# One block instead of three for a fused residual kernel with attention: shared PSUM banks and SBUF regions, first queries ahead of the first scores

## The chip, the cores and the metric

The kernel runs on one core of a Trainium2 chip. The metric is device time in microseconds (us) of one execution. Engines are named as in the profile: PE (TensorE matmuls), PEld (its weight loads), DVE (VectorE), ACT (ScalarE), POOL (GpSimd), SP (SyncE, which only issues DMAs here; "SPq" in the rows). "Hi" and "lo" are the two fp32r parts of an fp32 number; a product is three matmuls (hi·hi, lo·hi, hi·lo), summed in PSUM.

## The reference, cut to what matters

`x` is 8 × 128 × 512 in fp32. Four residual stages follow one another. Indices (`itok...`) pick an adapter for each of the 8 batches.

```
x += x @ W0[a0[b]].T                                   # L0: 512 x 512 of its own per batch
q,k,v = x @ wq,wk,wv + (x @ A[a1[b]]) @ B[a1[b]]       # L1: 32 query heads, 8 kv heads, D = 128
q,k = rope(q), rope(k)
p = softmax(where(causal & mask, q k^T / sqrt(128), min))
o = p v
x += o @ wo + (o @ ao[a1[b]]) @ bo[a1[b]]
x += (x @ B2[a0[b]].T) @ A2[a0[b]].T                   # L2, rank 16
x += x @ W3.T + b3 + 2 * (x @ A3[a3[b]]) @ B3[a3[b]]   # L3, rank 16
```

## The kernel before, in words

*Block one* (L0, and the first tiles of V): per batch, PE transposes x, multiplies by W0, and from batch four on (`LAG`) also does the V tile of an earlier batch with `v_tile` (L176-182), 8 tiles in all. It ends with PE at 97 us. In its last part ACT and DVE make the sine, cosine and mask tables.

*Block two* (L650-800, the projections): a loop over tiles n = 8..31, then four more. Tiles 8 to 15 are the second half of V, 16 to 31 are K (`project`, L70-83), 32 to 35 the queries of the first head for the first half of the tokens. A tile is 128 × 512 results in one of four banks `ps_p[n % 4]`. For a V tile, ACT copies the bank to `v_hi[n % 2]` (L733), DVE subtracts to get `v_lo[n % 2]` (L755), and SP stores both to HBM (`store_v`, L173). ACT may write `v_hi[n % 2]` again only once the stores of tile n-2 have landed (`v_out`). In the same loop ACT and DVE split the next block of weights out of `raw_w` and `raw_b` (L727, L729, L743, L167), and SP, behind the store of tile 11, loads `raw_w` for the block after (L148). For K and query tiles DVE multiplies by cosine and sine and POOL adds the two (L782) to `kr`, which SP stores to `k_rot`, or to `qt`. In the order of SP, behind the store of K tile 16, stand the loads of `wo` and of `ao` for head 0 (L646, 8 DMAs). POOL gathers the rows of `bo` and of L3's B (L773, L775; 16 DMAs) ahead of its first rotation.

*Block three* (attention and the rest): `over_heads` runs head 0, a hardware loop over heads 1 to 6, and head 7 written out as `last`. A head has 8 slots, one per batch. In a slot PE does the scores of its batch (L1403), a tile of queries (L76-81), the transposes of the previous batch's probabilities (`turn`, L1411), `outputs` of the batch before that (L1441-1445: o times wo and ao), and `values` of the previous batch (L1419-1421). DVE takes the scores' maxima (L1256), ACT the exponentials (L1055), POOL divides by the sums and adds the rotations of the queries; ACT and DVE split the transposed probabilities (`pt`: L1035, L1224) and the values' result (`ot`: L1041, L1228). `outputs(t)` waits for `ot(t)`.

In the last head the first four slots still make queries. In slots 4 to 7 `prepare(b)` works for the late stages: in slot 4 PE multiplies the L2 and L3 adapters (`m`) and DVE masks the result with `same` (`m_sb`, L1303), then in slot 5 PE folds it back and DVE adds it to `l3a_sel`, in slot 6 PE multiplies L2's A by W3 (`ps_c`). `m_sb` waits for `rows_in`, which counts `same` and the 8 `l2b_rows`. These two are loaded to `wo_raw`, which is free only late, and SP issues them behind 8 × (`l2b_sel`, `l2a_sel`) and 8 × `l3a_sel` (L981-994). After the last head: the sums `axo_n` are transposed (`turn_axo`, L1501), bo, L2 and L3 are multiplied, and x is stored.

## Time and profile before

| what | value |
|---|---|
| median of 3 runs | 783.78 us (782.24 to 786.15) |
| profiled execution, its own time | 783.69 us |
| its span, first to last instruction | 782.0 us |
| mean granted TensorE clock | 0.976 of full |
| PE busy | 719.9 us (92% of the span), 4388 matmul instructions |
| DVE / ACT / POOL busy | 537.2 / 327.0 / 291.0 us |
| mean share of the DMA engines, by the page's strip | from 0 to 9 tenths; 105 GB/s over the span |

The difference between 783.69 and 782.0 us lies around the span. PE is the engine with the most busy time; the 62 us in which it is not busy lie in a few places, which the views by stretch and the timelines of single engines show. A clock of 1.0 in a stretch is 2.4 GHz for PE, 0.5 is 1.2 GHz.

### The profile page before, as it was taken

To read this page: it belongs to the slowest core of one execution; us is meant where nothing else is said; L and a number is where in the kernel's file an instruction comes from. 1 tells how busy PE (TensorE), PEld (TensorE's weight loads), DVE (VectorE), ACT (ScalarE), POOL (GpSimd) and SP (SyncE) were. 2 spreads that over 40 slices of the span, in tenths; PEclk is the share of its full clock that TensorE was granted. 3 is DMA by queue.
4 is the path that set the end of the run, shared out by engine and by line. 5 is a ranking of instruction groups with operands and counts; after the bars stand their busy time and mean duration, and the time that the engine had idled before them with its cause. 6 is when DMAs were issued, how large, how long until landed. Compare 5 with 4: busy or idle time off the path is not lost.

```text
span 782.0 us, 14163 instructions
## 1 busy us (share of the span) xinstructions
PE 719.9 (92%) x4388; PEld 636.3 (81%) x4388; DVE 537.2 (69%) x1455; ACT 327.0 (42%) x980; POOL 291.0 (37%) x245
## 2 busy tenths in 40 slices
PE   3799958999789999999999999999999999968798
PEld 2678746887579989989998998998999899958686
DVE  4699434888586777677677768767676776834575
ACT  3563513110254454354445445436444543524332
POOL 3353122445362263344236235335423623423121
PEclk9999979999899999999999999999999999998999
DMA  7963277764014034023122403302412110527511
GB/s 229 347 215 123 81 202 225 224 251 170 19 55 128 2 128 129 2 74 134 47 57 70 127 0 127 127 0 74 134 47 73 54 47 7 123 55 97 67 42 67
DMA packets 60971, 81.81 MB, mean 105 GB/s; under 512 B 20438, under 2 KB 38102, under 8 KB 57350
## 3 DMA queue, kind: packets, MB, share of 16 engines
q1 hardware_dynamic: 60018, 80.04, 34.0%
q0 software_dynamic: 768, 1.25, 0.7%
q8 instruction: 18, 0.29, 0.2%
q14 instruction: 19, 0.16, 0.1%
q10 hardware_dynamic: 148, 0.07, 0.0%
HBM read 66.39 MB, written 15.47 MB: 105 GB/s over the span
## 4 chain that ended last, share of the span: by engine, by line
PE 65%; SPq 4%; DVE 3%; issue 2%; ACT 0%; DMA 0%; ACTq 0%
PE ps_wide L1441 8%; PE ps_wide L1445 8%; PE ps_wide L1443 7%; PE ps_q L76 7%; PE ps_q L78 7%; PE ps_q L77 7%; PE ps_s L1403 6%; PE ps_t L1411 3%; PE ps_o L1420 2%; PE ps_o L1419 2%; PE ps_o L1421 2%; PE ps_q L81 2%; PE ps_wide L1548 1%; PE ps_wide L1550 1%; PE ps_wide L1549 1%
## 5 line engine op out<-in xcount | busy, mean ns | idle before, releaser
L1170 POOL TENSOR_TENSOR prob<-prob,rinv 128x512 f32<-128x512 f32 x64 | 66.7, 1042 | 198.7 <-DVE rinv L1275 198.7
L1055 ACT ACTIVATE prob<-sm,nmax 128x128 f32<-128x128 f32 x256 | 99.8, 391 | 73.5 <-DVE nmax L1256 73.4
L1441 PE MATMUL ps_wide<-wt_x,v_hi 128*128 128x272 f32 x512 | 113.9, 304 | 10.4 <-DVE v_lo L1228 8.2
L1163 POOL TENSOR_TENSOR qt<-qc,qs 128x512 f32<-128x512 f32 x60 | 77.5, 1292 | 107.4 <-DVE qs L1211 107.4
L1445 PE MATMUL ps_wide<-wt_x,v_lo 128*128 128x272 f32 x512 | 107.5, 292 | 0.0
L1443 PE MATMUL ps_wide<-wt_lo,v_hi 128*128 128x240 f32 (+1 forms) x512 | 103.9, 285 | 0.0
L1041 ACT ACTIVATE v_hi<-ps_o 128x512 fp32r<-128x512 f32 x64 | 38.1, 596 | 155.2 <-PE ps_o L1421 155.2
L76 PE MATMUL ps_q<-x1t_hi,blk_hi 128*128 128x512 f32 x240 | 100.8, 420 | 0.0
L78 PE MATMUL ps_q<-x1t_hi,blk_lo 128*128 128x512 f32 x240 | 95.8, 399 | 0.0
L77 PE MATMUL ps_q<-x1t_lo,blk_hi 128*128 128x512 f32 x240 | 95.6, 398 | 0.0
L1441 PEld LDWEIGHTS ps_wide<-wt_x,v_hi 128*128 128x128 f32 x512 | 81.0, 192 | 14.4 <-DVE v_lo L1228 9.3
L1211 DVE TENSOR_TENSOR qs<-ps_q,sin_t 64x512 f32<-64x512 f32 x120 | 82.7, 689 | 3.7
L1443 PEld LDWEIGHTS ps_wide<-wt_lo,v_hi 128*128 128x128 f32 x512 | 81.8, 192 | 0.0
L1445 PEld LDWEIGHTS ps_wide<-wt_x,v_lo 128*128 128x128 f32 x512 | 80.6, 193 | 0.0
L1256 DVE CUSTOM_DVE_ANT_0 sm<-ps_s,maskbias 128x128 f32<-128x128 f32 x256 | 59.0, 286 | 29.6 <-issue 29.0
L1403 PEld LDWEIGHTS ps_s<-kt,qt 128*128 128x128 f32 x512 | 67.2, 193 | 11.4 <-issue 6.4
L1403 PE MATMUL ps_s<-kt,qt 128*128 128x128 f32 x512 | 68.4, 277 | 5.2 <-PEq L673 5.2
L1035 ACT ACTIVATE v_hi<-ps_t 128x512 fp32r<-128x512 f32 x64 | 38.2, 598 | 43.6 <-PE ps_t L1411 43.6
L1235 DVE TENSOR_TENSOR res<-ps_wide,res 128x272 f32<-128x272 f32 x128 | 50.0, 432 | 8.4 <-PE ps_wide L1445 8.4
L78 PEld LDWEIGHTS ps_q<-x1t_hi,blk_lo 128*128 128x128 f32 x240 | 45.6, 190 | 10.9
L1224 DVE TENSOR_TENSOR v_lo<-ps_t,v_hi 128x512 fp32r<-128x512 f32 x64 | 44.1, 689 | 14.0 <-ACT v_hi L1035 13.5
L77 PEld LDWEIGHTS ps_q<-x1t_lo,blk_hi 128*128 128x128 f32 x240 | 45.9, 191 | 8.5
(216 smaller groups left out, 1530.4 us busy)
## 6 DMA issues: line engine op xcount, KB each, us to landing
wo_raw<-in_L_cond_wo_l SPq DMA_DIRECT2D x8, 1024.0 KB, 4.8
raw_w<-in_L_cond_wq_l SPq DMA_DIRECT2D x8, 1024.0 KB, 5.2
raw_b<-in_L_cond_bq SPq DMA_DIRECT2D x64, 128.0 KB, 2.8
w_raw<-in_L_cond_weight_t SPq DMA_DIRECT2D x7, 1024.0 KB, 6.6
v_hi_d<-v_hi SPq DMA_DIRECT2D x16, 256.0 KB, 2.2
v_lo_d<-v_lo SPq DMA_DIRECT2D x16, 256.0 KB, 2.7
k_rot<-kr SPq DMA_DIRECT2D x16, 256.0 KB, 2.7
kt<-k_rot SPq DMA_DIRECT2D x16, 256.0 KB, 2.6
```

The source lines that it names most:

```text
L76: pe.matmul(bank[:, :], w_hi[:, k, cols], x1t_hi[:, k, tok], start=(k == 0), stop=False)
L77: pe.matmul(bank[:, :], w_hi[:, k, cols], x1t_lo[:, k, tok], start=False, stop=False)
L78: pe.matmul(bank[:, :], w_lo[:, k, cols], x1t_hi[:, k, tok], start=False, stop=False)
L1055: e = act.activation(prob[i][:, h, :], sm[:, h, :], ACT.Exp, bias=nmax[i][:, h:h + 1], scale=-1.0, accum_out=rsum[i][:, h:h + 1])
L1163: pool.tensor_tensor(qt[:, half, h, :], qc[:, :], qs[:, :], ALU.add).then_inc(q_done, 1)
L1170: pool.tensor_tensor(prob[i][:, :, :], prob[i][:, :, :], rinv[i][:, :].unsqueeze(2).broadcast_to([P, G, T]), ALU.mult).then_inc(prob_done, 1)
L1211: dve.tensor_tensor(qs[to:to + 64, :], ps_q[i][at:at + 64, :], sin_t[to:to + 64, tok], ALU.mult).then_inc(q_mult, 1)
L1256: m = dve.tensor_tensor_reduce(out=sm[:, h, :], in0=ps_s[i][:, h, :], in1=maskbias[:, b, :], scale=-1.0, scalar=3.0e38, op0=ALU.add, op1=A ...
L1403: mm = pe.matmul(ps_s[b % 2][:, h, :], qt[:, half, h, at:at + T], kt[:, b * T:(b + 1) * T], start=True, stop=True)
L1441: pe.matmul(ps_out[i][:, :], ot_hi[:, q], wo_x[:, h, wide], start=(h == 0), stop=False)
L1443: pe.matmul(bank, ot_hi[:, q], wo_lo[:, h, cols], start=False, stop=False)
L1445: mm = pe.matmul(ps_out[i][:, :], ot_lo[:, q], wo_x[:, h, wide], start=False, stop=(h == G - 1))
```

## The change

The three blocks become one. No engine waits for the others at the two seams; semaphores stand where a bank or a region passes from one use to the next.

- *Banks.* There are eight banks `bank[0..7]`. Stage one has `ps_x` = banks 0, 1 and `ps_y` = banks 2, 3; the projections' `ps_p` are banks 2, 3, 0, 1; attention has its scores in 4, 5, the transposes in 6, values in 7, queries in `ps_y` and outputs in `ps_x`.
- *SBUF.* Tiles that lived in different blocks share regions: `rot` (six tiles of 128 × 512) holds causal and mask tables, then k_cos, k_sin and kr, then attention's qc, qs, sm and prob, and in the end `axo_n`; `qt` lies where W0's raw weights were; `kt` and the values in the low and high parts of the K weights; `bo_raw` in one of the `blk_b`, the adapters of the late stages in `raw_b`.
- *Queries first.* In slot 0 of head 0, PE does the first tile of `queries` ahead of `scores(0)`; in all other slots the order stays.
- *Moved DMAs.* `ao` of head 0 is loaded behind the last rotated query tile, not behind K tile 16. `same` is loaded once at the start of the program, by POOL. In the last head SP issues `l2a` and `l3a` first (8 pairs), then bo's rows, then `l2b_sel` and `l2b_rows`.
- *Moved arithmetic in the last head.* `m` goes from slot 4 to slot 5 on PE, `m_sb` likewise on DVE, and waits for `same` alone; the fold goes from slot 5 to slot 7 on PE and behind the last `pt` on DVE. The memset of `axo_n` (L1292) goes from the start of attention on DVE to slot 4 of the last head. `l3a_hi` and `l2b_hi` go on ACT behind the heads, and their low parts with them.

The core of the diff (names and uses around it are left out where they only follow):

```diff
-        with ExitStack() as c:
-            k_cos = [sb(c, f"k_cos{i}", [P, HT]) for i in range(2)]
-            ps_p = [ps(c, f"ps_p{i}", [P, GW]) for i in range(4)]
-            with nc.Block() as block:
+            rot = sb(c, "rot", [P, 6, HT])
+            bank = [ps(c, f"bank{i}", [P, 512]) for i in range(8)]
+            ps_x, ps_y, ps_v = bank[0:2], bank[2:4], bank[5]
+            ps_p = ps_y + ps_x
+            v_bank = [ps_v] * LAG + [ps_p[n % 4] for n in range(LAG, B)]
+            ps_q, ps_t, ps_o, ps_wide = ps_y, bank[6], bank[7], ps_x
+            axo_n = rot[:, 0:2, :].rearrange("p i (b q a r) -> p (i b) q a r", q=4, a=2, r=R)
...
                         if n == VU:
                             load_wo(sp, 0)
-                            load_ao(sp, 0, 0)
-                            load_ao(sp, 0, 1)
...
+                    sp.wait_ge(k_done, VU + G)
+                    load_ao(sp, 0, 0)
+                    load_ao(sp, 0, 1)
...
                             if blk == 1:
+                                act.wait_ge(v_ready, UNITS)
...
                     def prepare(b):
                         if b == HALF:
-                            dve.wait_ge(rows_in, 16 * (B + 1))
-                            dve.wait_ge(m_ready, 1)
-                            dve.tensor_tensor(m_sb, ps_m, same, ALU.mult).then_inc(m_done, 1)
+                            dve.wait_ge(q_done, QUERIES)
+                            dve.memset(axo_n[:, :, :, :, :], 0.0).then_inc(axo_zeroed, 1)
                         elif b == HALF + 1:
                             dve.wait_ge(l2a_hi_done, 1)
                             dve.tensor_tensor(l2a_lo, l2a_sel[...], l2a_hi.bitcast(F32), ALU.subtract)
-                            dve.wait_ge(fold_ready, 1)
-                            dve.tensor_tensor(l3a_sel[...], by_batch(ps_fold[...]), l3a_sel[...], ALU.add)
+                            dve.wait_ge(same_in, 16)
+                            dve.wait_ge(m_ready, 1)
+                            dve.tensor_tensor(m_sb, ps_m, same[:, :], ALU.mult).then_inc(m_done, 1)
```

**How the rows move.** On PE around the first seam, the end of V tile 7, the join (branches) and the first matmuls of V tile 8 of the kernel before:

```order
L181 MATMUL ps_y1<-blk_hi0,x1t_lo 128x512
L182 MATMUL ps_y1<-blk_b0,axt_v 128x512
L248 UNCONDITIONAL_BRANCH
L784 UNCONDITIONAL_BRANCH
L179 MATMUL ps_p0<-wt_x,x1t_hi 128x512
```

The same place in the changed kernel (ps_y1 is bank1 there, ps_p0 is bank2):

```order
L172 MATMUL bank1<-blk_hi0,x1t_lo 128x512
L173 MATMUL bank1<-blk_b0,axt_v 128x512
L170 MATMUL bank2<-wt_x,x1t_hi 128x512
L171 MATMUL bank2<-wt_lo0,x1t_hi 128x512
L172 MATMUL bank2<-wt_x,x1t_lo 128x512
```

Both branches are gone, and tile 8 stands directly behind tile 7. On PE around the second seam, the end of the last projection (query tile 35), the join, and slot 0 of head 0, before:

```order
L78 MATMUL ps_p3<-x1t_hi,blk_lo0 128x512
L81 MATMUL ps_p3<-axt_q,blk_b0 128x256 x2
L673 UNCONDITIONAL_BRANCH
L1383 UNCONDITIONAL_BRANCH
L1403 MATMUL ps_s0<-kt,qt 128x128 x4
L76 MATMUL ps_q0<-x1t_hi,blk_hi0 128x512
```

The changed kernel there; bank2 is the query tile of slot 0, bank4 and bank5 the scores of slots 0 and 1 (`wt_lo1` holds kt), bank3 the query tile of slot 1:

```order
L72 MATMUL bank2<-x1t_hi,blk_lo0 128x512
L75 MATMUL bank2<-axt_q,blk_b0 128x256 x2
L1397 MATMUL bank4<-wt_lo1,qt 128x128 x4
L1397 MATMUL bank5<-wt_lo1,qt 128x128 x4
L70 MATMUL bank3<-x1t_hi,blk_hi0 128x512
```

The 13 matmuls of slot 0's query tile moved ahead of `scores(0)`, and follow the last projection with no join between. On DVE in slot 4 of the last head, before (`v_lo0` and `v_lo1` are the low parts of `pt` and `ot`, the line with `wo_raw` is `m_sb`):

```order
L1224 TENSOR_TENSOR v_lo0<-ps_t,v_hi0 128x512
L1235 TENSOR_TENSOR res<-ps_wide0,res 128x272
L1235 TENSOR_TENSOR res<-ps_wide1,res 128x272
L1303 TENSOR_TENSOR wo_raw<-ps_q0,wo_raw 128x128
L1228 TENSOR_TENSOR v_lo1<-ps_o,v_hi1 128x512
L1253 MEMSET gate 128x1
```

And in the changed kernel:

```order
L1012 TENSOR_TENSOR v_lo0<-bank6,v_hi0 128x512
L1023 TENSOR_TENSOR res<-bank0,res 128x272
L1023 TENSOR_TENSOR res<-bank1,res 128x272
L1089 MEMSET rot 128x1024
L1016 TENSOR_TENSOR v_lo1<-bank7,v_hi1 128x512
L1041 MEMSET gate 128x1
```

The low part of `ot` (L1228, now L1016) no longer stands behind `m_sb`, but behind the memset of `axo_n`.

## Rows read from the trace of the kernel before

**Rows 1.** Windows by stretch: start:end, length, busy of PE, PEld, DVE, ACT, POOL, clock, DMA share, GB/s.
```profile
97.00:107.00 10.00, 0.36 (x2) 0.21 (x2) 3.21 (x4) 1.42 (x4) 0.00 (x0) 0.67 0.80 233
...
227.00:687.00 460.00, 459.89 (x3019) 418.46 (x3018) 334.08 (x1067) 210.92 (x706) 186.03 (x155) 1.00 0.24 75
```

**Rows 2.** Timeline of PE at the first seam: start, duration, instruction, [idle before <-releaser].
```profile
96.55 0.40 PE L181 MATMUL ps_y<-blk_hi,x1t_lo 128*128 128x512 f32 x1
96.79 0.40 PE L182 MATMUL ps_y<-blk_b,axt_v 128*128 128x512 f32 x1
106.82 0.77 PE L179 MATMUL ps_p<-wt_x,x1t_hi 128*128 128x512 f32 x1 [9.64 <-PEq L248]
...
110.72 0.40 PE L179 MATMUL ps_p<-wt_x,x1t_hi 128*128 128x512 f32 x1
```

**Rows 3.** Timeline of SP in the projections (DMA issues).
```profile
100.12 4.95 SPq L154 DMA_DIRECT2D raw_b<-in_L_cond_bk  x8
...
122.25 0.37 SPq L173 DMA_DIRECT2D v_hi_d<-v_hi  x1
123.22 0.57 SPq L148 DMA_DIRECT2D raw_w<-in_L_cond_wk_l  x1
...
143.79 4.46 SPq L646 DMA_DIRECT2D ao_raw<-in_L_cond_ao_l  x8
```

**Rows 4.** Stores of v_lo, 105 to 132 us, then the one at 105.9.
```profile
DMA to landing us min/median/max: 2.6/4.1/7.5
...
DMA to landing us min/median/max: 4.9/4.9/4.9
```

**Rows 5.** Timeline of ACT, the copy of V tile 14; POOL, its first gather.
```profile
133.25 0.60 ACT L733 ACTIVATE v_hi<-ps_p 128x512 fp32r<-128x512 f32 x1 [5.20 <-DMA v_lo_d<-v_lo]
...
108.57 0.51 POOL L773 DMA_DIRECT2D bo_sel<-in_L_cond_bo  x1 [15.99 <-issue]
```

**Rows 6.** Timeline of PE, K tile 16 and a later K tile.
```profile
135.29 0.50 PE L76 MATMUL ps_p<-x1t_hi,blk_hi 128*128 128x512 f32 x1 [2.36 <-DVE blk_b L167]
...
185.94 0.49 PE L76 MATMUL ps_p<-x1t_hi,blk_hi 128*128 128x512 f32 x1 [1.54 <-DVE blk_b L167]
```

**Rows 7.** Timeline of PE in the last head: outputs, then the matmul after them.
```profile
702.28 0.82 PE L1441 MATMUL ps_wide<-wt_x,v_hi 128*128 128x272 f32 x2 [5.75 <-DVE v_lo L1228]
...
707.83 1.10 PE L1480 MATMUL ps_q<-wo_raw 128*128 128x128 f32 x8
...
722.39 0.52 PE L1441 MATMUL ps_wide<-wt_x,v_hi 128*128 128x272 f32 x2 [2.45 <-DVE v_lo L1228]
...
731.40 0.75 PE L1501 MATMUL ps_q<-ident,axo_n 128*128 128x128 f32 x4 [3.85 <-DVE axo_n L1321]
```

**Rows 8.** Timeline of PE at the second seam and in slots 0 and 1.
```profile
197.95 0.40 PE L81 MATMUL ps_p<-axt_q,blk_b 128*128 128x256 f32 x2
203.53 1.20 PE L1403 MATMUL ps_s<-kt,qt 128*128 128x128 f32 x4 [5.18 <-PEq L673]
...
217.25 0.47 PE L1419 MATMUL ps_o<-v_hi 128*128 128x512 f32 x1 [2.39 <-DVE v_lo L1224]
...
222.31 0.50 PE L1441 MATMUL ps_wide<-wt_x,v_hi 128*128 128x272 f32 x2
```

**Rows 9.** Timeline there: POOL's last rotation, DVE's memset, rotation and next maxima.
```profile
200.60 1.26 POOL L782 TENSOR_TENSOR qt<-k_cos,k_sin 128x512 f32<-128x512 f32 x1 [1.76 <-DVE k_sin L766]
...
204.06 0.91 DVE L1292 MEMSET axo_n<- 128x1024 f32 x1 [0.16 <-issue]
...
212.74 0.06 DVE L1253 MEMSET gate<- 128x1 f32 x1
```

**Rows 10.** Timeline of SP in the last head, and of DVE at m_sb.
```profile
679.32 0.56 SPq L985 DMA_DIRECT2D l2a_sel<-in_L_cond_A_l  x1
...
682.81 7.96 SPq L988 DMA_DIRECT2D l3a_sel<-in_L_cond_lora_As_l  x8
...
701.34 0.29 DVE L1303 TENSOR_TENSOR wo_raw<-ps_q,wo_raw 128x128 f32<-128x128 f32 x1 [6.90 <-DMA wo_raw<-in_L_cond_B]
```

More of the change, by code:

```diff
@@ new lines, in program @@
+            same = sb(c, "same", [P, P])
+            gate = sb(c, "gate", [P, 1])
+            nmax = [sb(c, f"nmax{i}", [P, G]) for i in range(2)]
+            rsum = [sb(c, f"rsum{i}", [P, G]) for i in range(2)]
+            rinv = [sb(c, f"rinv{i}", [P, G]) for i in range(2)]
+            xt = sb(c, "xt", [P, 4, KC * T], F32R)
+            wt_hi1 = sb(c, "wt_hi1", [P, KC, HID], F32R)
+            wt_lo1 = sb(c, "wt_lo1", [P, KC, HID], F32R)
+            w0_raw = [qt[:, i, :, :] for i in range(2)]
@@ L210, in program @@
-            ps_at = ps(c, "ps_at", [P, 3, T])
+            rot_flat = rot[:, :, :].rearrange("p i t -> p (i t)")
+            a_raw = rot_flat[:, 0:4 * KC * 3 * R].rearrange("p (i k n r) -> p i k n r", i=4, k=KC, r=R)
+            causal = rot[:, 2, 0:T]
+            mask_u8 = rot[:, 3, 0:NT // 4].bitcast(U8)
+            small = blk_b[1][:, :, :].rearrange("p c n -> p (c n)")
+            A_COLS = KC * 3 * R
+            a_hi, a_lo = ([small[:, (2 * j + i) * A_COLS:(2 * j + i + 1) * A_COLS].rearrange("p (k n r) -> p k n r", k=KC, r=R)
+                           for i in range(2)] for j in range(2))
@@ new lines, in program @@
+            kv_v_hi = sem(c, "v_hi_done2")
+            kv_v_lo = sem(c, "v_lo_done2")
+            scaled = sem(c, "scaled")
+            k_mult = sem(c, "k_mult")
+            k_done = sem(c, "k_done")
+            k_out = [sem(c, f"k_out{i}") for i in range(2)]
+            BLOCKS = 2 * VB
+            VU = VB * UNITS
+            N0 = UNITS
+            wq_raw, bq_raw, wq_hi, wq_lo, bq_pack = raw_w, raw_b, blk_hi[0], blk_lo[0], blk_b[0]
+            wo_x, wo_hi, wo_lo = wt_x, blk_hi[1], blk_lo[1]
@@ new lines, in program, with load_late @@
+            nar_ready = sem(c, "nar_ready")
+            h_hi_done = sem(c, "h_hi_done")
+            h_lo_done = sem(c, "h_lo_done")
+            late_hi_done = sem(c, "late_hi_done")
+            late_lo_done = sem(c, "late_lo_done")
+            wide_ready = sem(c, "wide_ready")
+            y_done = sem(c, "y_done")
+            y_out = sem(c, "y_out")
+            QUERIES = B * (KVH - 1) + HALF
+            def load_late(dma, src, at, done):
+                for quad in range(4):
+                    row = 2 * R * quad + at
+                    dma.dma_start(late_raw[row:row + R, :, :], src.rearrange("b r n -> r b n")).then_inc(done, 16)
@@ new lines, in by_batch, with of_nar, flat, ao_of @@
+            def by_batch(tile):
+                return tile.rearrange("p k (b r) -> p b k r", r=R)
+            def of_nar(tile, which):
+                return tile[:, :, :, which, :].rearrange("p b k r -> p (b k) r")
+            def flat(tile):
+                return tile[:, :, :, :].rearrange("p b k r -> p (b k) r")
+            def ao_of(b, part):
+                at = part * R + b % 2 * (2 * R + HID)
+                return wo_x[:, :, at:at + R]
+            def over_heads(eng, slots):
+                slots(0, True, False)
+                with eng.Fori(1, KVH - 1) as g:
+                    slots(g, False, False)
+                slots(KVH - 1, False, True)
@@ L415, in _ @@
+                    for b in range(B):
+                        sp.wait_ge(y_done, b + 1)
+                        sp.dma_start(out[b], x_row(b)).then_inc(y_out, 16)
+                    sp.wait_ge(y_out, 16 * B)
                 @block.scalar
@@ L501, in _ @@
+                    x2t(0)
+                    act.wait_ge(late_in, 64)
+                    act.wait_ge(c_in, 64)
+                    late_part(0)
+                    for b in range(B):
+                        if b == 0:
+                            axo_part(1)
+                        if b + 1 < B:
+                            x2t(b + 1)
+                        narrow(b)
+                        if b + 1 < B:
+                            late_part(b + 1)
                 @block.vector
@@ new lines, in turn_ax @@
+                    def turn_ax(b):
+                        pe.wait_ge(axn_done, 4 * b + 4)
+                        if b == 0:
+                            pe.wait_ge(ident_ready, 1)
+                        else:
+                            pe.wait_ge(axt_done, 3 * b)
+                        for n in range(3):
+                            mm = pe.matmul(ps_at[:, n, :], axn[b % 2][:, n, :, :, :].rearrange("p a b r -> p (a b r)"),
+                                           ident_r[:, :], start=True, stop=True)
+                        mm.then_inc(axt_ready, 1)
```

1172 lines of the change are left out of this document (538 added, 634 removed).

## The prediction, made before the changed kernel was run

> **What bounds the kernel now.** I read the windows by stretch first, then the timelines of PE, SP, DVE, ACT and POOL around the stretches in which PE is idle. In the loop over heads PE is busy 459.89 of 460 us, and DVE, the next engine, 334.08 [rows 1]: there only PE's own work counts, and the change leaves it as it is. In the 10 us at the first seam PE is busy 0.36 us [rows 1], and its next matmul has stood idle for 9.64 us behind a branch [rows 2]. At the second seam it is 5.18 us [rows 8]. In the last head `outputs` waits 5.75, later 2.45 and 3.85 us [rows 7]. So the time to be had lies in three places; each is followed from what arrives last there. The profiled execution took 783.69 us, the median of the runs is 783.78: the sum made against the one holds for the other.
>
> **First seam.** Removed is the join: V tile 8 could start at 97.0, one matmul spacing (96.79 − 96.55 = 0.24) after 96.79, instead of at 106.82 [rows 2]. The nine matmuls from 106.82 to 110.72 also took 3.90 us where nine at 0.24 take 2.2, so 1.7 us of half clock goes too. PE alone would come out of the eight V tiles at 97.0 + 8 × 13 × 0.24 = 122.0, and start K tile 16 there instead of at 135.29 [rows 6]: 13.3 earlier.
>
> But the V tiles are not PE's alone. ACT may write v_hi(n) only when the stores of tile n−2 have landed, and SP's list is not moved here. The stores of tile 7 stand behind the 4.95 us of `raw_b` issues from 100.12 [rows 3]; the last one, issued at 105.9, took 4.9 us and landed at 110.8 [rows 4]. That doesn't depend on the join, so v_hi(9) is at 110.8 in both kernels. From there: copy and subtraction about 1.3, stores issued at 112.1, landed some 2.6 to 4.1 us later [rows 4], say 115.1; v_hi(11), again 1.4, its stores at 116.5. The `raw_w` load follows its store by 123.22 − 122.25 = 0.97 [rows 3]: 117.5 instead of 123.22. Before, v_hi(14) came 133.25 − 123.22 = 10.0 us after that load, since it waits for stores that share the DMA engines with it [rows 3, 5], and PE's K tile 16 came 135.29 − 133.25 = 2.04 later [rows 5, 6]. At those distances tile 16 starts at 129.5, 5.8 earlier. Some of the 10.0 was crowding by POOL's 16 gathers, which began at 108.57, 15.99 us after its last work [rows 5]; without the join they are over by some 110. I take 8.5 for the 10.0: tile 16 at 128.0, 7.3 earlier. The ends are 5.8 and 13.3.
>
> At 7.3, PE stands still for 128.0 − 122.0 = 6.0 us, in several pieces or one. After 9.64 idle the half clock cost 1.7 [rows 2]; after 5.75 idle the twelve pairs of matmuls from 702.28 to 707.83 took 5.55 for 12 × 0.24 = 2.9, so 2.65 [rows 7]. I subtract 2.2 (0 to 2.65).
>
> The `ao` loads, 4.46 us of SP ahead of the second `k_rot` store [rows 3], leave the chain of the K tiles, which stall PE once by 1.54 [rows 6]. Their own loads are wanted only in slot 1 of attention. I take 0.5 (0 to 1.5). Sum of the first seam: 7.3 − 2.2 + 0.5 = 5.6 (3.4 to 13.8).
>
> On what stores cost beside a load: rows 4 show 2.6 us in the quiet and up to 7.5 beside the 1 MB load. The Trainium skill (DMA: Bandwidth & Descriptors, "Issuing engines are not separate DMA queues") says that transfers begun by different engines interleave on the same 16 DMA engines. By that rule moving POOL's gathers matters to SP's stores and the chain above holds; were it otherwise, 8.5 would be 10.0 and the sum 1.5 less.
>
> **Second seam.** Before: last matmul at 197.95, the rotation of the last query tile ended at 200.60 + 1.26 = 201.86 [rows 8, 9], scores(0) at 203.53, the next maxima at 212.74 [rows 9], values(0) at 217.25, outputs(0) at 222.31 [rows 8]. After: queries(0) runs at 198.2 to 201.3 under the last rotation, scores(0) and scores(1) start at 201.9. The maxima of slot 0 end at some 203.9 (four of 0.3), DVE is free, as the memset of 0.91 [rows 9] has gone; exponentials to 205.6, the rotation of queries(0) beside them to 208.0, the maxima of slot 1 at 208.1 instead of 212.74. Values(0) keeps its distance to these (217.25 − 212.74 = 4.5): 212.6, which is 4.65 earlier. But PE has made its query tiles by about 207.7 and then waits 4.9 us for the transposed probabilities. If the clock drops there as in rows 7, outputs(0) starts at 220.4 rather than 217.7, which leaves 1.9, and with the 0.5 of small waits in slots 0 and 1 gone, 2.4. I take 2.4 (1.7 to 4.9).
>
> **Last head.** Before: DVE waited 6.90 us for `l2b_rows` ahead of `m_sb` at 701.34 [rows 10], the low part of `ot` stood behind it on DVE, and outputs(3) started at 702.28 [rows 7]. SP came there through 8 pairs at 1.77 (679.32 is one), 8 `l3a` in 7.96 us, and 8 `l2b_rows` [rows 10]. After, `m_sb` is one slot later and waits for `same` alone, loaded long before. DVE in slot 4 has the memset of 0.91 [rows 9] instead, under the copy of `ot`'s high part. So the idle 5.75 us ahead of outputs(3) go, and its twelve pairs run at full clock, another 2.65: 8.4. The 0.9 us of `m` (the row of 1.10 at 707.83, less its overlap) no longer stand between outputs(3) and outputs(4): 9.3. What is late next is `l2a` and `l3a` for `m` in slot 5. Their 8 pairs at 1.1 for `l3a` + 1.3 for `l2a` = 2.4 are 19.2 us from about 667, issued by 686 and landed by 690. They are wanted a slot after 696: hidden. So are bo's rows, at 688, and `l2b_rows`, at 701 and wanted in slot 7. But `m_sb` and `l2a_lo` stand in slot 5 ahead of the low part of ot(4), and hold outputs(4) for about 1.6 us: 7.7. In slot 5 `m` takes on PE what the fold did, and the wait of 2.45 ahead of outputs(5) stays, or shrinks by little: 722.39 becomes about 715. The transposes of `axo_n`, which waited 3.85 at 731.40 [rows 7], gain some tenths more, since `ot` of the last but one batch goes ahead of the sums on DVE and the fold's sum behind the last `pt`. The last loads (`c_rows`) lie inside what PE does then, with little to spare. I take 7.9 (6.5 to 9.5).
>
> **Sum.** 5.6 + 2.4 + 7.9 = 15.9, so 783.69 − 15.9 = 767.8. The ends of all terms together give 3.4 + 1.7 + 6.5 = 11.6 (772.1) and 13.8 + 4.9 + 9.5 = 28.2 (755.5).
>
> **Rivals.**
>
> *The chain of stores does not bind.* The stores land at their quickest, the gathers were what slowed them, and PE comes straight through: 13.3 + 0.5 + 2.4 + 7.9 = 24.1, 759.6. For it: 2.6 us is the quickest landing [rows 4]. Against: v_hi(9) at 110.8 and three more rounds of two tiles at 4.3 each already reach 123.7, past PE's 122.0.
>
> *The clock stays up in the new gaps.* Then 2.2 and about 2.3 come back: 763.3. For it: the gaps may be split among tiles, and at 185.94 a wait of 1.54 was followed by a matmul of 0.49, near the usual 0.40 [rows 6]. Against: 5.75 was enough in rows 7. The Trainium skill (TensorE: Matmul & The Clock Gate, Part 1) has the half rate as the default state that activity releases; by it both gaps cost, as in the sum.
>
> *The first seam gives nothing.* If the load of `raw_w` is held by something that doesn't move (it wants `raw_lo` of its block, made by DVE, whose tables fill it after 97 us), tile 16 keeps near 135.3, and 2.4 + 7.9 remain: 773.4. For it: the DMA share there is 0.80 [rows 1], and the chain starts from an unmoved landing. Against: from 110.8 on, every step in the chain above is one that the join delayed.
>
> *Slower: the shared region.* The rotations, the scores' copies and the probabilities now lie in one region `rot`, beside each other. If this slowed DVE, ACT or POOL so that each slot of some 8 us became 0.3 longer, 56 slots would give 16.8, and the time is 784.6. It decides only once the chain of DVE passes PE: DVE has 126 us idle in 460 [rows 1], some 2.2 a slot, so its instructions must become longer by more than a third, and nothing in the trace shows one that depends on where its operand lies.
>
> **How the numbers follow.** Forecast 0.60, no binding chain 0.15, clock stays 0.10, first seam nothing 0.10, slower region 0.05. The range has to reach from past the third to between the forecast and the loosest ends: 758 to 775 leaves out half of the first rival and the last one. About 0.5% (3.9 us) is what a measurement of this kernel can tell from no change. All cases but the last are faster by more: 0.95; of the last 0.02 lies within 0.5% and 0.03 beyond.
>
> **What would show it.** PE's first matmul of V tile 8 within a microsecond of tile 7's last; v_hi(9) at about 111, K tile 16 near 128, with waits for the copies of V before it and a few matmuls of 0.63 behind them. Values(0) 10.7 us after scores(0) instead of 13.7, and one gap of PE of about 5 us before it. No wait of `outputs` above 2 us in the last head. PE without a gap in the loop over heads, as now [rows 1]. I am wrong if K tile 16 doesn't come earlier by at least 5 us, if the loop's heads change, or if the last head has a new wait for `l3a` or for bo's rows.

## The result, and the profile after

The changed kernel takes 772.62 us (median of 4 runs, 772.02 to 773.42) against 783.01 us of the kernel before; the ratio is 0.9873, with a 95% interval of 0.983 to 0.9915. It is faster by some 10 us, inside the forecast range (758 to 775), but 4.8 us short of the 767.8 that were forecast, and 0.5 us beyond the 772.1 at which the forecast's own terms all stand at their low ends. Its profiled execution spans 771.4 us, against 782.0.

PE at the first seam. The timeline's columns are start, duration, instruction, and in brackets the idle time before it with what ended it:

```profile
98.52 0.39 PE L173 MATMUL bank<-blk_b,axt_v 128*128 128x512 f32 x1
98.75 0.40 PE L170 MATMUL bank<-wt_x,x1t_hi 128*128 128x512 f32 x1
...
133.07 0.80 PE L70 MATMUL bank<-x1t_hi,blk_hi 128*128 128x512 f32 x1 [7.95 <-DVE blk_b L158]
133.66 0.63 PE L71 MATMUL bank<-x1t_lo,blk_hi 128*128 128x512 f32 x1
...
185.88 0.50 PE L70 MATMUL bank<-x1t_hi,blk_hi 128*128 128x512 f32 x1 [1.92 <-DVE blk_b L158]
```

The join is gone: V tile 8 starts 0.23 us after tile 7's last matmul, where it was 10.03 [rows 2]. But stage one itself ended 1.7 us later here (98.52 against 96.79), K tile 16 starts at 133.07 instead of 135.29 [rows 6], behind a new wait of 7.95 us and at half clock (0.63 a matmul), and query tile 32 starts at 185.88, as good as before (185.94 [rows 6]). The windows by stretch (start:end, length, busy time of PE, PEld, DVE, ACT, POOL, PE's clock, DMA share, GB/s):

```profile
98.75:133.00 34.25, 25.18 (x105) 19.10 (x103) 14.30 (x21) 10.01 (x19) 5.91 (x12) 0.96 0.79 228
133.00:185.80 52.80, 50.89 (x224) 41.36 (x224) 45.63 (x64) 8.81 (x17) 24.40 (x15) 0.96 0.67 219
...
223.70:683.70 460.00, 460.00 (x3016) 418.22 (x3015) 334.01 (x1067) 210.69 (x706) 185.90 (x155) 1.00 0.24 73
```

In the V tiles PE is busy 25.2 of 34.3 us, and the DMA engines are at 0.79. In the K tiles DVE is busy 45.6 of 52.8. The loop over heads has no gap of PE, as before [rows 1]. The kernel before, from K tile 16 to query tile 32:

```profile
135.29:185.94 50.65, 49.11 (x224) 39.98 (x224) 44.06 (x63) 8.84 (x17) 23.04 (x14) 1.00 0.69 233
```

So of the 2.1 us by which this stretch is longer now, 1.8 are PE busy at half clock behind the wait of 7.95 (50.89 against 49.11), and 0.4 the longer wait at its end (1.92 against 1.54); between the two PE doesn't wait. What PE waited for in the V tiles is in the chain of waits (start, length, what):

```profile
101.24 0.52 SPq L139
101.86 0.48 SPq L145
...
107.59 0.39 SPq L164
108.04 5.80 DMA v_lo_d<-v_lo
113.92 0.61 ACT v_hi L693
114.56 0.70 DVE v_lo L975
115.28 0.37 SPq L164
115.69 4.64 DMA v_lo_d<-v_lo
120.41 0.61 ACT v_hi L693
121.05 0.70 DVE v_lo L975
121.77 0.37 SPq L164
122.18 0.51 SPq L164
122.73 0.57 SPq L139
...
123.85 7.10 DMA v_lo_d<-v_lo
131.03 0.61 ACT v_hi L693
131.66 0.69 DVE v_lo L975
132.36 0.67 DVE blk_b L158
133.07 0.80 PE bank L70
```

It is the chain of the forecast: the stores of tile 7 behind `raw_b` (L145), v_hi(9), stores of tile 9, v_hi(11), stores of tile 11, the load of `raw_w` (L139), the stores of tile 12 beside it, v_hi(14), K tile 16. Its links up to the load of `raw_w` are longer than forecast. ACT's copies of tiles 9 to 12 and 14:

```profile
113.92 0.60 ACT L693 ACTIVATE v_hi<-bank 128x512 fp32r<-128x512 f32 x1 [2.99 <-DMA v_lo_d<-v_lo]
115.60 0.60 ACT L693 ACTIVATE v_hi<-bank 128x512 fp32r<-128x512 f32 x1 [0.56 <-DMA v_lo_d<-v_lo]
120.41 0.60 ACT L693 ACTIVATE v_hi<-bank 128x512 fp32r<-128x512 f32 x1 [3.69 <-DMA v_lo_d<-v_lo]
121.90 0.60 ACT L693 ACTIVATE v_hi<-bank 128x512 fp32r<-128x512 f32 x1 [0.37 <-DMA v_lo_d<-v_lo]
...
131.03 0.60 ACT L693 ACTIVATE v_hi<-bank 128x512 fp32r<-128x512 f32 x1 [4.83 <-DMA v_lo_d<-v_lo]
```

In the kernel before, the copy of tile 9 waited for PE:

```profile
114.86 0.60 ACT L733 ACTIVATE v_hi<-ps_p 128x512 fp32r<-128x512 f32 x1 [1.89 <-PE ps_p L182]
```

PE at the second seam and at slots 0 and 1:

```profile
197.90 0.40 PE L75 MATMUL bank<-axt_q,blk_b 128*128 128x256 f32 x2
198.14 0.39 PE L70 MATMUL bank<-x1t_hi,blk_hi 128*128 128x512 f32 x1
...
201.88 0.38 PE L1397 MATMUL bank<-wt_lo,qt 128*128 128x128 f32 x1 [0.55 <-POOL qt L1218]
...
212.62 0.77 PE L1413 MATMUL bank<-v_hi,wt_hi 128*128 128x512 f32 x1 [4.71 <-DVE v_lo L1012]
...
219.02 0.49 PE L1435 MATMUL bank<-wt_x,v_hi 128*128 128x272 f32 x2
```

Scores(0) and values(0) stand where they were forecast (201.9 and 212.6), outputs(0) at 219.02 instead of 222.31 [rows 8]. The last head, PE's four starts of rows 7, the first without its wait of 5.75:

```profile
693.30 0.52 PE L1435 MATMUL bank<-wt_x,v_hi 128*128 128x272 f32 x2 [0.49 <-DVE v_lo L1016]
...
700.83 0.52 PE L1435 MATMUL bank<-wt_x,v_hi 128*128 128x272 f32 x2 [1.40 <-DVE v_lo L1016]
...
712.31 0.52 PE L1435 MATMUL bank<-wt_x,v_hi 128*128 128x272 f32 x2 [2.53 <-DVE v_lo L1016]
...
722.35 0.66 PE L1501 MATMUL bank<-ident,rot 128*128 128x128 f32 x4 [3.23 <-DVE rot L1114]
```

And DVE there, where the memset stands in the place of `m_sb` [rows 10] and ahead of the low part of `ot`:

```profile
690.84 0.79 DVE L1023 TENSOR_TENSOR res<-bank,res 128x272 f32<-128x272 f32 x2 [1.29 <-PE bank L1439]
691.79 0.91 DVE L1089 MEMSET rot<- 128x1024 f32 x1 [0.16 <-issue]
692.61 0.63 DVE L1016 TENSOR_TENSOR v_lo<-bank,v_hi 128x512 fp32r<-128x512 f32 x1
```

**All runs by stretch.** Stage one does not take the same time in every execution, whatever comes behind it: in the fourteen profiles its last matmul (V tile 7) lies between 93.3 and 98.5 us. So each stretch is measured between two matmuls of the same profile. "V7" is the last matmul of V tile 7, "K16" and "Q32" the first of those tiles, "out(t)" the first of `outputs(t)`; all from PE's timeline, in us.

| kernel | V7 | V7 to K16 | V7 to Q32 | Q32 to out(8) | out(8) to out(58) | out(58) to out(60) | out(60) to last |
|---|---|---|---|---|---|---|---|
| before | 96.79 | 38.50 | 89.16 | 101.35 | 403.12 | 20.64 | 67.42 |
| before, again | 96.53 | 37.97 | 88.23 | 100.95 | 403.11 | 21.12 | 67.48 |
| changed | 98.52 | 34.55 | 87.37 | 98.07 | 403.64 | 13.24 | 66.95 |
| join one back | 94.44 | 38.57 | 91.12 | 98.70 | 403.54 | 13.25 | 68.41 |
| join two back | 93.33 | 34.74 | 85.95 | 105.59 | 403.60 | 13.25 | 66.96 |
| rows wait back | 95.89 | 35.23 | 88.26 | 98.06 | 403.63 | 24.71 | 68.51 |
| store first | 93.35 | 30.92 | 83.98 | 99.69 | 403.63 | 13.24 | 66.97 |
| four V buffers | 97.76 | 27.15 | 84.45 | 98.51 | 403.65 | 13.24 | 68.24 |
| gathers early | 95.69 | 33.85 | 89.20 | 100.35 | 403.72 | 14.78 | 66.98 |
| scores first | 94.44 | 32.74 | 87.82 | 101.10 | 403.72 | 14.78 | 66.98 |
| both V edits | 96.82 | 25.54 | 79.40 | 99.05 | 403.61 | 14.80 | 66.97 |
| K edit | 94.36 | 35.17 | 88.85 | 98.28 | 403.60 | 13.25 | 66.99 |
| V and K edits | 96.04 | 25.11 | 77.02 | 99.66 | 403.69 | 13.25 | 66.95 |
| the same, POOL later | 97.39 | 25.85 | 74.82 | 98.31 | 403.69 | 13.24 | 66.95 |

Before to changed, along its rows: +1.73 (stage one) − 1.79 (to Q32) − 3.28 (to out(8)) + 0.52 (the loop) − 7.40 (last head) − 0.47 = −10.7, and the two spans differ by 10.6.

### The profile page after: what moved, and what is told of

It reads as the page before. It is cut to its first block, busy times and chain, and to the rows that moved or that the text cites. A ratio compares the mean times of both kernels' runs of the same rounds, so it can differ in the third digit from the quotient of the medians.

```text
span 771.4 us, 14127 instructions
## 1 busy us (share of the span) xinstructions
PE 718.3 (93%) x4388; PEld 633.4 (82%) x4388; DVE 540.0 (70%) x1455; ACT 326.8 (42%) x980; POOL 292.6 (38%) x246
## 4 chain that ended last, share of the span: by engine, by line
PE 77%; DVE 8%; DMA 6%; SPq 3%; issue 3%; ACT 2%; POOL 1%; ACTq 0%; POOLq 0%; DVEq 0%
PE bank L1435 9%; PE bank L1439 8%; PE bank L70 8%; PE bank L72 8%; PE bank L71 8%; PE bank L1437 8%; PE bank L1397 7%; PE bank L1405 3%; DMA qt<-in_L_cond_weight_t 2%; DMA v_lo_d<-v_lo 2%; PE bank L75 2%; PE bank L1413 2%; PE bank L1414 2%; PE bank L1415 2%; DVE blk_b L158 1%
## 5 line engine op out<-in xcount | busy, mean ns | idle before, releaser
L742 ACT ACTIVATE rot<-rot,nmax 128x128 f32<-128x128 f32 x256 | 99.7, 391 | 82.8 <-DVE nmax L1044 82.8
L70 PE MATMUL bank<-x1t_hi,blk_hi 128*128 128x512 f32 x288 | 119.7, 416 | 9.9 <-DVE blk_b L158 9.9
L1435 PE MATMUL bank<-wt_x,v_hi 128*128 128x272 f32 x512 | 112.6, 301 | 6.4 <-DVE v_lo L1016 4.4
L72 PE MATMUL bank<-x1t_hi,blk_lo 128*128 128x512 f32 x288 | 114.6, 398 | 0.0
L71 PE MATMUL bank<-x1t_lo,blk_hi 128*128 128x512 f32 x288 | 114.5, 398 | 0.0
L1439 PE MATMUL bank<-wt_x,v_lo 128*128 128x272 f32 x512 | 106.4, 289 | 0.0
L1437 PE MATMUL bank<-wt_lo,v_hi 128*128 128x240 f32 (+1 forms) x512 | 102.9, 282 | 0.0
L1435 PEld LDWEIGHTS bank<-wt_x,v_hi 128*128 128x128 f32 x512 | 79.8, 190 | 10.0 <-DVE v_lo L1016 5.1
L999 DVE TENSOR_TENSOR rot<-bank,sin_t 64x512 f32<-64x512 f32 x120 | 82.7, 689 | 3.7
L1437 PEld LDWEIGHTS bank<-wt_lo,v_hi 128*128 128x128 f32 x512 | 80.7, 189 | 0.0
```

What stands on the lines that cost most here:

```text
L70: pe.matmul(bank[:, :], w_hi[:, k, cols], x1t_hi[:, k, tok], start=(k == 0), stop=False)
L71: pe.matmul(bank[:, :], w_hi[:, k, cols], x1t_lo[:, k, tok], start=False, stop=False)
L72: pe.matmul(bank[:, :], w_lo[:, k, cols], x1t_hi[:, k, tok], start=False, stop=False)
L742: e = act.activation(prob[i][:, h, :], sm[:, h, :], ACT.Exp, bias=nmax[i][:, h:h + 1], scale=-1.0, accum_out=rsum[i][:, h:h + 1])
L999: dve.tensor_tensor(qs[to:to + 64, :], ps_q[i][at:at + 64, :], sin_t[to:to + 64, tok], ALU.mult).then_inc(q_mult, 1)
L1435: pe.matmul(ps_out[i][:, :], ot_hi[:, q], wo_x[:, h, wide], start=(h == 0), stop=False)
```

## The experiments

**Join one back.** The bodies of the engines are cut in two at the first seam, and run in two blocks:

```diff
-            with nc.Block() as block:
-                @block.sync
-                def _(sp):
+            if True:
+                def body_sp(sp):
...
+                    yield
                     for n in range(N0, BLOCKS * UNITS):
...
+            for _part in range(2):
+                with nc.Block() as block:
+                    block.sync(run("sp", body_sp))
```

`yield` marks the seam in each engine's body, and `run` carries a body on from where it stopped; the other four engines have the same edit.

> The changed kernel with the join of all engines put back at the first seam alone (between stage one and the projections); everything else as changed. Theory A: the first seam gave next to nothing, since the stores of V and, behind them, the loads of the K blocks set when K tile 16 and the query tiles start; then this one takes 772 to 775 us, and PE reaches query tile 32 (185.88 us in the changed kernel) within 1.5 us of that. Rival B: the seam gave the 5.6 us that were forecast and something else took them; then it takes 777 to 779 us and reaches that tile at 190 to 192.

Measured: 774.85 us (768.65 to 775.19, ratio 0.9895, 0.9846 to 0.9943), Q32 at 185.56 us. PE waits at the seam as before:

```profile
104.63 0.77 PE L170 MATMUL bank<-wt_x,x1t_hi 128*128 128x512 f32 x1 [9.81 <-PEq L1585]
```

By its two numbers theory A holds. But stage one ended 4 us earlier here than in the changed kernel. Counted from V7, the join costs 4.0 us at K16 (38.6 against 34.55) and 3.7 at Q32 (91.1 against 87.4). The three profiles with the join (the kernel before twice, and this one) have 88.2 to 91.1 at Q32, mean 89.5; those that leave all of this part as changed (changed, join two back, rows wait back, scores first) have 86.0 to 88.3, mean 87.4. So the first seam is worth about 2 us by the means, not 5.6; the two groups touch at 88.2, so how far from 0 it lies at Q32 is less sure than the 4 us at K16, where they are 38.0 to 38.6 and 32.7 to 35.2.

**Join two back**, the same cut at the second seam.

> The changed kernel with the join put back at the second seam alone (between the projections and attention), queries still ahead of the first scores. Theory A: this seam is worth what the traces show between query tile 32 and outputs(0), 3.2 us; the queries now stand behind the join as well, ahead of scores(0), so it loses that and up to 4 more for the query tile at half clock: 775.5 to 779 us. Rival B: POOL's rotations and the exponentials set the start of attention anyway: 772 to 774 us.

Measured: 778.44 us (773.96 to 780.73 in 10 runs, ratio 0.9952, 0.9928 to 0.9975). Theory A's range (the profiled execution, at 773.96, is the fastest of the ten; its stage one ended at 93.33). Q32 to out(8) grows by 7.5 us:

```profile
197.30 0.77 PE L70 MATMUL bank<-x1t_hi,blk_hi 128*128 128x512 f32 x1 [5.60 <-PEq L1585]
```

**Scores first.** One block, but the first queries behind the first scores:

```diff
                             if first and b == 0:
-                                pe.wait_ge(k_mult, 3 * (VU + 1))
-                                queries(t, 1, b)
                                 pe.wait_ge(k_done, VU + G)
```

> The changed kernel with the first queries behind the first scores again, as before the change, in the same single block. Theory A: PE waits for the last rotation (201.86 us) and then runs the query tile, 3.1 us, more at half clock; scores(1), and with them all of slot 1, come later; 3 to 4.5 us lost at outputs(0): 775.5 to 777.5 us. Rival B: the second seam gained by the missing join alone: 772 to 774 us.

Measured: 773.34 us (772.26 to 775.56, ratio 0.9857, 0.9802 to 0.9911), below theory A's range, and by the time alone rival B. The stretch says otherwise: Q32 to out(8) takes 101.10, the 101.35 and 100.95 of before, not 98.07. PE stands for the last rotation and has nothing else:

```profile
199.78 2.07 PE L1397 MATMUL bank<-wt_lo,qt 128*128 128x128 f32 x8 [3.57 <-POOL qt L1218]
```

But 1.5 of the 3.0 us come from ahead of the seam. In this profile PE waits 4.10 us ahead of Q32 and makes the query tiles at half clock; its last projection starts 13.55 us after Q32, and in the changed kernel 12.02 (197.90 − 185.88), as before the change (197.95 − 185.94):

```profile
182.26 0.57 PE L70 MATMUL bank<-x1t_hi,blk_hi 128*128 128x512 f32 x1 [4.10 <-DVE blk_b L158]
...
195.81 0.40 PE L75 MATMUL bank<-axt_q,blk_b 128*128 128x256 f32 x2
```

From that last projection to out(8), with nothing of the first seam in it, the four cases are, in us:

| | scores first | queries first |
|---|---|---|
| join | 89.34 and 88.94 (before) | 93.57 (join two back) |
| no join | 87.56 (scores first) | 86.05 (changed); 86.04 to 87.05 in the ten profiles of this form, mean 86.41 |

So taking the join away alone gives some 1.6 us, and the new order behind it some 1.2 more. The 1.2 are little more than the 1.0 by which the ten differ; cleaner is values(0), which comes 1.7 us later here than in all ten, where its distance to the last projection is the same to 0.02 us. Beside a join the new order loses 4.4 us. The whole gain of the seam needs both edits. The cell without join and with the scores first rests on one profile. This profile's time isn't longer by as much, since its stage one ended 4.1 us earlier; its out(58) to out(60) is another 1.5 us longer, by chance of the clock (below). What the other three runs did in these stretches isn't on record.

**Rows wait back.** DVE in slot 4 of the last head waits for `l2b_rows` again:

```diff
                         if b == HALF:
+                            dve.wait_ge(rows_in, 16 * B)
                             dve.wait_ge(q_done, QUERIES)
```

> The changed kernel in which DVE in slot 4 of the last head waits again for the 8 l2b_rows (which land at 700.2 us here) ahead of what it does there. Theory A: this wait was what the last head lost before; outputs(3) starts at about 701.5 instead of 693.3, at half clock, and most of the 7.9 us that the last head gained is lost again: 779 to 781 us. Rival B: the last head gained by the moved DMAs and folds, not by the wait: less than 3 us lost, 773 to 776 us.

Measured: 783.36 us (779.9 to 788.96 in 10 runs; ratio to the kernel before 1.0023, 0.9997 to 1.0049): all of the gain is gone, 10.7 us against the changed kernel, beyond the 779 to 781 us that theory A had.

```profile
700.48 0.82 PE L1436 MATMUL bank<-wt_x,v_hi 128*128 128x272 f32 x2 [9.42 <-DVE v_lo L1016]
```

The 9.42 us and the half clock behind them make out(58) to out(60) 11.5 us longer. A wait for these rows alone is enough to lose what the last head gained. It is dearer here than it was before (9.42 against 5.75): PE comes to it 4.6 us earlier in the same head (out(58) at 685.84 against 690.41), but the rows, which now stand behind bo's rows too, land only 2.6 us earlier (698.70 against 701.31). Whether the wait could have gone without the new order of the DMAs was not tried.

**The kernel before, again.**

> The kernel before, profiled once more, to tell how far stage one differs between executions of one kernel. If the 1.7 us by which stage one ended later in the changed kernel are chance, the last matmul of V tile 7 lies anywhere from 93 to 99 us here; if the change made stage one longer, it lies within 0.5 us of 96.8 or below.

Measured: 782.69 us, V7 at 96.53. That lies in both ranges of the expectation, so it doesn't decide. The twelve profiles of the changed kernel and its variants lie between 93.3 and 98.5, mean 95.7, on both sides of the two of before. The start of stage one is the same in all of them but for the place of one buffer and one small load (gathers early has POOL's gathers in it too), so the +1.73 us of the changed kernel's profile is best read as chance; two profiles of before don't prove it.

**Store first.** On SP the stores of V tile 7 ahead of the `raw_b` loads:

```diff
                             load_block_w(sp, 2)
-                            load_block_b(sp, 2, picks)
+                    load_block_b(sp, 2, picks)
```

> The changed kernel with one step moved on SP: the stores of V tile 7 go ahead of the 8 loads of raw_b for the first K block, not behind them. Theory A: the landing of these stores (113.8 us) starts the chain of V tiles; issued at about 103.2 they land by 108 or 109, v_hi(9) follows, and K tile 16 starts 3 to 5 us earlier than 133.07; of that 1 to 3 us are left at query tile 32: 770 to 772 us. Rival B: they land no earlier behind the 1 MB load of raw_w (109.3), or the later stores lose it again: 772 to 773.5 us, and K tile 16 at 132 to 133.

Measured: 769.16 us (766.12 to 773.01, ratio 0.9863, 0.9828 to 0.9897). V7 to K16 is 3.6 us shorter, to Q32 3.4. As theory A has it, the landing of these stores (104.5 instead of 113.8) starts the chain. Of the gain, 3.4 us are left at Q32, more than the 1 to 3 that theory A gave, and 1.5 of them go to half clock in the query tiles.

**Four V buffers.**

```diff
-                            act.wait_ge(v_out[n % 2], 32 * (n // 2))
-                            act.activation(v_hi[n % 2][:, :], ps_p[n % 4][:, :], ACT.Copy).then_inc(kv_v_hi, 1)
+                            if n < UNITS + 2:
+                                act.wait_ge(v_out[n % 2], 32 * (n // 2))
+                            elif n >= UNITS + 4:
+                                act.wait_ge(v_out2[n % 4], 32)
+                            act.activation(more[0][n % 4], ps_p[n % 4][:, :], ACT.Copy).then_inc(kv_v_hi, 1)
```

The stores, DVE's subtraction and the last waits follow to the new buffers.

> The changed kernel with four buffers for the V tiles of the projections instead of two (the new two lie where stage one had the transposed x), so that v_hi(n) waits for the stores of tile n-4. Distances are counted from the last matmul of V tile 7, since stage one's own length differs by up to 5 us between executions. Theory A: the round of store and landing sets the V tiles; with four buffers K tile 16 starts 27 to 31 us after that point instead of 34.6, and query tile 32 83 to 85 us instead of 86 to 88: 769 to 771 us. Rival B: the loads for the K block set tile 16: 33 to 35 us and no gain.

Measured: 765.48 us (763.14 to 771.12, ratio 0.9745, 0.9691 to 0.9799). V7 to K16 falls to 27.15 us, within 2.9 of PE's own 8 × 3.03 = 24.2 (a tile is 13 matmuls, 0.233 apart). To Q32 only 2.9 of the 7.4 us are left: PE now waits in the K tiles (4.27 us ahead of one at 153.62).

**Gathers early.** POOL's 16 gathers, two in each step of stage one from the second on, instead of behind it.

> The changed kernel with POOL's 16 gathers of bo and L3's B spread over stage one, two in each of its steps, instead of behind it (94 to 112 us). Theory A: they crowd the loads and stores of the first seam; without them the stores of V tile 7 land in 4 to 5 us instead of 5.8 and K tile 16 starts 1 to 3 us earlier, counted from V tile 7: 770 to 772 us. Rival B: they only move the crowding into stage one, which is bound by loads until 65 us: 772 to 774 us.

Measured: 775.03 us (772.39 to 776.07, ratio 0.9866, 0.9811 to 0.992). No gain: K16 comes 0.7 us earlier from V7, Q32 1.8 later, and the stores of V tile 7 land in 5.5 us (5.80 in the changed kernel). Rival B, or nothing at all.

**Both V edits** (store first and four buffers).

> The changed kernel with both V edits: four buffers for the V tiles, and the stores of V tile 7 ahead of the raw_b loads. Theory A: each took some 3.5 to 7.5 us off the way from V tile 7 to K tile 16, but the K tiles then have a floor of their own, so together they give K tile 16 at 25 to 27 us after V tile 7 (27.15 with four buffers alone) and query tile 32 still at 83 to 85: 764 to 768 us. Rival B: what they save adds up at query tile 32: 80 to 82 us there, 761 to 764 us.

Measured: 764.79 us (761.31 to 767.32, ratio 0.9745, 0.97 to 0.979), Q32 79.40 us after V7. The time lies in theory A's range, but Q32 comes earlier than in either theory: the savings more than add up (3.4 and 2.9 alone, 8.0 together). There is no fixed floor at 83 in the K tiles.

**K edit.** Four buffers for the rotated K tiles, `kt` and v of head 0 loaded six tiles later (the stores and the last waits, which follow, are left out):

```diff
-                        if n == VU + 4:
+                        if n == VU + 10:
...
-                        if 2 <= m < VU:
-                            pool.wait_ge(k_out[i], 16 * (m // 2))
-                        rotated = kr[i] if m < VU else qt[:, 0, m - VU, :]
+                        if 4 <= m < VU:
+                            pool.wait_ge(k_out[m % 4], 16 * (m // 4))
+                        rotated = kr4[m % 4] if m < VU else qt[:, 0, m - VU, :]
```

> The changed kernel with the K tiles' chain loosened alone: four buffers for the rotated K tiles instead of two, and the six loads of kt and v for head 0 issued six tiles later. Theory A: the k_rot store that landed 6.4 us late behind these loads, and POOL's wait for it, held the raw_b loads and with them PE at query tile 32; that tile then comes 84 to 86 us after V tile 7 instead of 87.7 (mean of the unjoined ones), 769 to 771 us. Rival B: DVE sets the K tiles (three multiplications and a split per tile, and a split that takes 1.87 us instead of 0.75 whenever POOL adds beside it): 87 to 88.5 us, 772 to 774 us.

Measured: 771.26 us (769.35 to 776.16, ratio 0.9847, 0.9802 to 0.9892), Q32 88.85 us after V7. Theory A falls: in the changed kernel's profile a landing of `k_rot` of 6.39 us was on the chain to Q32, but with it gone DVE is there. PE waits 0.89 us twice, both times for `blk_b`, where it waited 1.92 once.

**V and K edits.**

> The changed kernel with both V edits and the K edit. Theory A: V tiles and K tiles are two chains one behind the other, each with a floor by stores; with both loosened PE alone sets the pace: 24 tiles of 3.03 are 72.8 us from V tile 7 to query tile 32, some 76 to 80 with what waits remain, 758 to 763 us. Rival B: DVE's floor in the K tiles stays: 82 to 84 us, 764 to 767 us.

Measured: 758.02 us (755.69 to 761.95, ratio 0.9671, 0.9628 to 0.9715), Q32 77.0 after V7, as theory A had it, and the time at the low end of its range. This is 3% faster than the kernel before, and the interval lies below that of the changed kernel. What PE still waits for are two splits of `blk_b`; DVE's timeline has three long ones of eight (the next expectation, written from this profile, says four):

```profile
141.72 1.88 DVE L158 SCALAR_TENSOR_TENSOR blk_b<-blk_b,rope_cols,raw_b 128x512 fp32r<-128x512 f32 x1
...
164.15 0.75 DVE L158 SCALAR_TENSOR_TENSOR blk_b<-blk_b,rope_cols,raw_b 128x512 fp32r<-128x512 f32 x1
167.19 1.89 DVE L158 SCALAR_TENSOR_TENSOR blk_b<-blk_b,rope_cols,raw_b 128x512 fp32r<-128x512 f32 x1
171.15 1.85 DVE L158 SCALAR_TENSOR_TENSOR blk_b<-blk_b,rope_cols,raw_b 128x512 fp32r<-128x512 f32 x1
```

POOL's additions beside the last three of these:

```profile
164.19 1.86 POOL L1228 TENSOR_TENSOR rot<-rot 128x512 f32<-128x512 f32 x1 [1.18 <-DVE rot L996]
167.23 1.29 POOL L1228 TENSOR_TENSOR rot<-rot 128x512 f32<-128x512 f32 x1 [1.18 <-DVE rot L996]
171.19 1.26 POOL L1228 TENSOR_TENSOR qt<-rot 128x512 f32<-128x512 f32 x1 [2.67 <-DVE rot L996]
```

Where the addition takes 1.86 the split beside it takes 0.75, and the other way round.

**POOL later.** The same kernel, with those additions behind the split:

```diff
+                        if m + 1 < VU and (m + 1) % UNITS >= KC:
+                            pool.wait_ge(kv_raw_lo, m + 1 + VU - N0 + 1)
```

> The kernel with both V edits and the K edit (e10) and one wait more: POOL's addition for a K tile waits for DVE's next split where that is one of blk_b, so that the two no longer run side by side. In e10 four of the eight such splits in the K tiles took 1.85 to 1.89 us instead of 0.75, beside an addition of 1.29, and PE waited 0.89 and 1.99 us behind them. Theory A: the collision on what DVE and POOL share to reach SBUF costs this; all splits take 0.75, both waits of PE shrink below 0.3, and query tile 32 comes at 74 to 75.5 us after V tile 7 instead of 77.0: 755.5 to 757 us. Rival B: the long splits have another cause, or POOL's later additions delay the stores as much: 76.5 to 78 us, 757.5 to 760 us.

Measured: 759.37 us (755.64 to 761.02, ratio 0.9697, 0.9651 to 0.9742), Q32 74.82 us after V7, 2.1 above PE's own 24 × 3.03 = 72.7. All eight splits are short now, by the view of that line:

```profile
L158 DVE SCALAR_TENSOR_TENSOR blk_b<-blk_b,rope_cols,raw_b x8: 750/751/753, 137.7 to 171.4; 128x512 fp32r<-128x512 f32 x8
```

The changed kernel has 743/752/1883 ns there (minimum, median, maximum). The mechanism of theory A is shown, and with it 2.2 us of the stretch in one profile of each kernel; its time is not: the median is no better than without the wait, with both intervals overlapping.

## Why the prediction was right or wrong

**Last head: right.** 7.9 us were forecast; out(58) to the last matmul became 7.9 shorter (88.06 to 80.19). The wait on DVE was the cause (rows wait back). That it is 7.9 to the tenth is luck: in the other kernels with this last head the same stretch takes 80.2 to 81.8, and 88.6 in the second profile of before, so the gain is 6.3 to 8.4. Outputs(3), (4), (5) and the transposes came 9.0, 10.2, 10.1 and 9.05 us earlier; less the 2.8 by which out(58) was ahead these are 6.2, 7.4, 7.3 and 6.2. (The forecast had the transposes gain more than outputs(5), not less; what comes behind them made it up.) The new waits of 1.40 and 2.53 are the forecast 1.6 and the one that "stays".

**Second seam: right.** 2.4 us (1.7 to 4.9) were forecast, 3.2 and 3.3 measured at outputs(0) and out(8), 2.7 between the means from the last projection to out(8). The forecast gave it to the two edits together, and the four cases bear that out: the missing join alone gives some 1.6, and the new order beside a join loses 4.4. The gap of 4.71 us ahead of values(0) is the forecast 4.9, with half clock behind it.

**First seam: wrong in size, 5.6 forecast, about 2 measured** (1.8 in the two profiles, 2.1 between the means). That is below the low end that the forecast gave it, 3.4. The low end itself was added up wrong (5.8 − 2.65 + 0 = 3.15, and the high one 13.3 − 0 + 1.5 = 14.8, not 13.8), which changes nothing here: 3.15 is above the measured 1.8 too. By the prediction's own sign, K tile 16 at least 5 us earlier, this part is wrong: it came 2.2 us earlier, and 4.0 counted from V7. The chain was the right one, and so was the rival rejected (PE straight through). In the forecast's own terms, 7.3 at K tile 16 was 4.0; the 2.2 of half clock were 1.8; and the 0.5 gained in the K tiles was a loss of 0.4: 1.8 in all. Nearly all that is missing is in the first term, and there in two landings:
- *"The stores of tile 7 landed at 110.8. That doesn't depend on the join."* They landed at 113.8. Of the 3.0 us between, 1.7 are stage one's later end, on which all of SP's list hangs, 0.4 the issue and 0.9 the landing (5.80 for 4.9). Why that landing is longer stays open: with the gathers out of the way it was still 5.5 (gathers early).
- *Rounds of two tiles at 4.3 us.* The first took 6.5 (115.28 to 121.77): the landing 4.64 and not 3.0, the rest in the issue of the second store and the waits between. In the kernel before, ACT's copies of V tiles 9 to 13 waited for PE (1.9 us each, 3.02 apart), and landings of 2.7 to 4.1 us were hidden; in the changed one all from tile 9 on wait for a landing. Most come in pairs (9 with 10, 11 with 12, 14 with 15, some 1.5 us apart), so the stores crowd each other, and those of tiles 9 to 13 land in 2.8 to 7.1 us. That the crowding makes them late is argued, not tried by itself.

The last step, "8.5 for the 10.0", was good: 8.3 (122.73 to 131.03). Its reason holds as well: the second load of `raw_w` for K landed in 7.8 to 8.2 us in the three profiles with the join, where POOL's gathers run until 124 to 127 beside it, and in 6.6 to 6.9 in the seven without the join that have two V buffers.

*What tile 16 gains, the query tiles gain* held but for 0.4 us in the changed kernel (1.92 for 1.54 of wait at Q32, above); the 0.5 by the `ao` loads doesn't show. It would have held less had the V tiles been as quick as forecast: with four V buffers K16 came 7.4 us earlier and Q32 2.9, since the K tiles have chains of their own, `k_rot` behind six loads and splits on DVE that POOL's addition makes 1.1 us longer. The kernel with all of them loosened reaches 74.8.

Counted from V7 the links miss 0.4 + 0.9 + 2.2 − 0.2 = 3.3 us, which is 7.3 less 4.0. So the step that failed is to take the landings of the stores over from the profile of before (4.9 and 3.0 us), where the stores went out 3.0 us apart, into a kernel whose stores follow each other more closely. Measured from V7 the gain was 4 us at K16 and 2 at Q32.

**Luck in the sum.** The measured time lies in the stated range (758 to 775), but not between the ends that the terms add up to (772.1 and 755.5; rightly added 772.3 and 754.5). The range holds it since it was drawn out past the rival of 773.4.

**The loop: not quite as it was.** Out(8) to out(58) takes 403.5 to 403.7 us in the changed kernel and all its variants, and 403.1 in both profiles of before: 0.5 us lost in 50 slots, 10 ns in each. The rival of the shared region had 0.3 us a slot; whether this is a thirtieth of it or something else was not tried.

**The rivals.** The clock did fall in the gaps that were forecast. "The first seam gives nothing" had 773.4 us, the nearest number, for a reason that wasn't so: the profile's time is made up of 1.8 us of seam, against which stand 1.7 of a late stage one and the loop's 0.5. The lock between DVE and POOL agrees with what the Trainium skill says (SBUF — State Buffer, "SBUF: two separate sides"): a VectorE operation with two inputs in SBUF and a GpSimd operation that reads SBUF exclude each other, and the one that comes second stands still. Here one of the two took 1.8 to 1.9 us where alone it takes 0.75 (DVE) or 1.29 (POOL), little less than their sum of 2.04, and the other took its usual time. Which of them came second the rows don't show: in the pairs shown above DVE's start is recorded 0.04 us ahead each time, whichever is the long one. The multiplications of DVE, with one input in PSUM, kept their 0.69 beside an addition.
